# Rows added inside the output projection by an identity product, a shorter root chain, and four layer-norm tiles moved to ScalarE

## The reference

```python
def _layernorm(x, axis=-1, eps=1e-05):
    m = jnp.mean(x, axis=axis, keepdims=True)
    v = jnp.var(x, axis=axis, keepdims=True)
    return (x - m) / jnp.sqrt(v + eps)

x = x + _L0_attn_ref(_layernorm(x, axis=-1), ...)            # "own", causal, 16 heads; ends in out @ out_w + out_b
x = x + _L0_xattn_ref(_layernorm(x, axis=-1), ctx_1024, ...) # "cross", 154 keys; ends in out @ Wo + bo
x = x + _L0_ffn_ref(_layernorm(x, axis=-1), ...)             # "feed", quantised, with a depthwise convolution
x = x + _L1_attn_ref(_layernorm(x, axis=-1), ...)            # "second", 16 heads; ends in out @ w_out.T + b_out
x = x + _L1_xattn_ref(_layernorm(x, axis=-1), ctx_1024, ...) # "wide", one head
x = x + _L1_ffn_ref(_layernorm(x, axis=-1), ...)             # experts, top 2 of 16, and a shared one
return x
```

## Time and profile before

| | us |
|---|---|
| median of 3 runs | 3818.49 (3815.27 to 3821.42) |
| the profiled execution | 3815.54 |
| its span, first to last instruction | 3814.1 |
| TensorE busy (products) | 3274.6 (86% of the span) |
| VectorE busy | 2484.7 (65%) |
| ScalarE busy | 1735.8 (46%) |
| GpSimd busy | 546.1 (14%) |
| mean granted TensorE clock | 0.886 of full |

### The profile page before, as it was taken

One profiled execution on the slowest core, in us unless ns is written; L12 is line 12 of the kernel. 1 busy time (PEld: TensorE's weight loads), 2 busy tenths in 40 slices (PEclk: granted clock), 3 DMA queues, 4 the chain that ended last, 5 costly groups with the idle time before them and its releaser, 6 DMA issues. The chain is left out here.

```text
span 3814.1 us, 47638 instructions
## 1 busy us (share of the span) xinstructions
PE 3274.6 (86%) x17904; PEld 1798.5 (47%) x17904; DVE 2484.7 (65%) x4712; ACT 1735.8 (46%) x2434; POOL 546.1 (14%) x990
## 2 busy tenths in 40 slices
PE   5997679979999768988999975998898977799889
PEld 3443332358644333236864433323686433322378
DVE  5856678646685577854667547884566755688456
ACT  2553436633345443653345444465334544546532
POOL 0111010014111101002401110100241010010033
PEclk8898779979989777998998977799898997789989
DMA  3211011013021101101312010110231111021022
GB/s 122 43 32 35 0 26 34 9 47 112 23 51 23 35 1 34 26 9 62 107 25 47 15 35 1 34 34 1 76 93 38 35 21 29 1 42 26 1 89 91
DMA packets 119366, 149.24 MB, mean 39 GB/s; under 512 B 25445, under 2 KB 77159, under 8 KB 118835
## 3 DMA queue, kind: packets, MB, share of 16 engines
q1 hardware_dynamic: 119115, 145.95, 15.9%
HBM read 75.46 MB, written 4.46 MB: 21 GB/s over the span
## 5 line engine op out<-in xcount | busy, mean ns | idle before, releaser
L694 DVE TENSOR_REDUCE small<-psum 128x1 f32<-128x512 f32 (+6 forms) x1856 | 1148.6, 657 | 332.3 <-PE psum L571 293.8
L660 ACT ACTIVATE work<-psum 128x1024 f32<-128x1024 f32 (+5 forms) x1024 | 921.4, 935 | 502.5 <-PE psum L598 252.5
L571 PE MATMUL psum<-work 96*128 96x512 bf16 (+4 forms) x2688 | 729.1, 341 | 137.8 <-issue 59.6
L1607 PE MATMUL psum<-rounded_work 128*128 128x512 f32 (+1 forms) x3456 | 621.0, 343 | 4.4 <-ACT work L1671 4.4
L594 PE MATMUL psum<-work 99*128 99x512 bf16 (+4 forms) x2048 | 590.0, 372 | 8.8 <-DMA work<-work 6.5
L1607 PEld LDWEIGHTS psum<-rounded_work 128*128 128x128 f32 x3456 | 543.5, 193 | 80.9 <-ACT work L1671 6.3
L571 PEld LDWEIGHTS psum<-work 96*128 96x128 bf16 x2688 | 244.7, 103 | 695.4 <-DVE small L694 362.8
L626 PE MATMUL psum<-work 128*32 128x512 f32 (+4 forms) x4480 | 545.9, 540 | 1.6 <-ACT work L660 1.4
L594 PEld LDWEIGHTS psum<-work 99*128 99x128 bf16 (+1 forms) x2048 | 182.7, 99 | 216.9 <-ACT work L660 64.8
L1679 ACT CAST rounded_work<-work 128x512 fp32r<-128x512 f32 x144 | 89.3, 620 | 352.1 <-DVE work L1714 324.6
L724 POOL CAST small<-small 128x16 bf16<-128x16 f32 x96 | 18.8, 196 | 1418.0 <-issue 1104.0
(11 more groups left out here) (271 smaller groups left out, 3914.4 us busy)
## 6 DMA issues: line engine op xcount, KB each, us to landing
work<-work SPq DMA_DIRECT2D x320, 192.0 KB, 4.3
work<-combine SPq DMA_DIRECT2D x64, 512.0 KB, 4.0
work<-in_w_gate SPq DMA_DIRECT2D x64, 128.0 KB, 3.5
work<-in_w_up SPq DMA_DIRECT2D x64, 128.0 KB, 3.4
work<-in_w_down SPq DMA_DIRECT2D x64, 128.0 KB, 3.8
work<-in_x SPq DMA_DIRECT2D x10, 512.0 KB, 5.0
out<-x SPq DMA_DIRECT2D x8, 512.0 KB, 2.9
work<-work SPq DMA_DIRECT2D x64, 28.9 KB, 2.0
```

The source lines that it names most:

```text
L571: ins = nc.tensor.matmul(dst[:, c * n:(c + 1) * n], A.q_pair[0:ROWS, slot, h, P * i:P * (i + 1)], A.k_of(pair, h)[0:ROWS, s0:s0 + n], star ...
L660: nc.scalar.activation(probs[0:size, n % 4, :, 0:P * many], banks(2 * (n % 2), 2)[0:size, :, 0:P * many], ACT.Exp, scale=DH ** -0.5).then_ ...
L694: nc.vector.tensor_reduce(tops[:, pair % 2, places[0]:places[-1] + 1:step], src, AX.X, ALU.max) \
L1607: ins = nc.tensor.matmul(dst, a_parts[i], b_parts[j], start=start and n == 0, stop=stop and n == 2, skip_group_check=True)
```

## The change

- Out projections: GpSimd's sum leaves `x` plus bias in `x` as before. TensorE now multiplies two tiles of it at a time by the identity (`rows_tensor`, 128 by 512 float32) into bank j with `start=True`, and the projection's products of both tiles are accumulated on top. Four such products: the first ahead of the last pair's spin, the second behind it, the third behind the last turn, the fourth ahead of the last two tiles. VectorE takes the statistics straight from PSUM, and ScalarE copies each finished bank to `x` (`sum_scalar`). VectorE's adds are gone, and so are TensorE's waits for them, in `cross_tensor` and `wide_tensor` too.
- Root chain: variance plus epsilon is folded into ScalarE's square root (scale 0.25 and a bias of epsilon/4, which makes half the root), and the refining step into two combined instructions; the clamp, one sum and one halving go. This holds for every norm.
- The first four tiles of the norms own, cross, feed and second are normed by ScalarE (`norm_rows_scalar`, Identity with a scale and a bias per partition), after VectorE has written -mean times rstd for the half (mark `scaled`). ScalarE's order is given in `out_scalar`.
- GpSimd's bias sums of cross and second are issued after its top part of pair 2 in these heads.
- The marks are regrouped on semaphores `vector_norm` and `scalar_norm`.

```diff
 def norm_half(tag, i0, rows=None):
+    norm_variance(tag, i0, HT)
+    norm_root(tag, i0, HT)
+    if by_scalar(tag, i0):
+        nc.vector.scalar_tensor_tensor(out=root_parts(i0, HT)[1], in0=mean_of(i0, HT), scalar=-1.0, in1=rstd[:, i0:i0 + HT],
+                                       op0=ALU.mult, op1=ALU.mult).then_inc(*up("vector_norm", "scaled", tag))
+    else:
+        for j in range(i0, i0 + HT):
+            norm_rows(tag, j, rows)
...
-            own(ins)
-            nc.vector.tensor_scalar(root_parts(i0, n)[2], variance_of(i0, n), LN_EPS, None, ALU.add).then_inc(*up("variance", tag, i0))
+            ins.then_inc(*up("vector_norm", "variance", tag, i0))
...
-            dve.wait_ge(*at("root", tag, i0))
-            own(nc.vector.tensor_scalar(s0, s0, 1e-18, None, ALU.max))
+            dve.wait_ge(*at("scalar_norm", "root", tag, i0))
             own(nc.vector.reciprocal(s1, s0))
-            own(nc.vector.tensor_tensor(s1, s1, s2, ALU.mult))
-            own(nc.vector.tensor_tensor(s0, s0, s1, ALU.add))
-            own(nc.vector.tensor_scalar(s0, s0, 0.5, None, ALU.mult))
+            own(nc.vector.scalar_tensor_tensor(out=s2, in0=variance_of(i0, n), scalar=LN_EPS, in1=s1, op0=ALU.add, op1=ALU.mult))
+            own(nc.vector.scalar_tensor_tensor(out=s0, in0=s2, scalar=0.25, in1=s0, op0=ALU.mult, op1=ALU.add))
             own(nc.vector.reciprocal(rstd[:, i0:i0 + n], s0))
...
+        def norm_rows_scalar(tag):
+            act.wait_ge(*at("vector_norm", "scaled", tag))
+            for j in range(HT):
+                if tag in SUMMED:
+                    act.wait_ge(*at("added", tag, j // 2))
+                nc.scalar.activation(xn[:, j, :], x[:, j, :], ACT.Identity, scale=rstd[:, j:j + 1], bias=root_parts(0, HT)[1][:, j:j + 1]) \
+                    .then_inc(*up("scalar_norm", "normed", tag, j))
...
                 elif kind == "spin":
                     pair, = key
+                    if pair == PAIRS_OF_HEADS - 1:
+                        rows_tensor(A, 0)
...
                     ins.then_inc(*up("spun", a, pair))
+                    if pair == PAIRS_OF_HEADS - 1:
+                        rows_tensor(A, 1)
...
+                    if pair == 2 and bias is not None:
+                        out_gpsimd(A, bias)
...
+        def rows_tensor(A, j):
+            if j == 0:
+                pe.wait_ge(*at("filled", A.tag))
+            nc.tensor.matmul(bank(j), ident[:, :], x[:, 2 * j:2 * j + 2, :].rearrange("p i d -> p (i d)"), start=True, stop=False, skip_group_check=True)
+
         def out_tensor(A, tag, w):
+            rows_tensor(A, 2)
             pe.wait_ge(*at("out_turned", A.tag, 1, 1))
-            for i in range(NT):
-                if i >= 4:
-                    pe.wait_ge(*at("added", tag, i - 4))
-                project(bank(4 + i % 4)[:, 0:D], lambda k: oT[:, k, P * i:P * (i + 1)], w).then_inc(*up("out_projected", tag, i))
+            for j in range(NT // 2):
+                if j == 3:
+                    rows_tensor(A, 3)
+                for i in (2 * j, 2 * j + 1):
+                    for k in range(KD):
+                        ins = nc.tensor.matmul(bank(j)[:, D * (i % 2):D * (i % 2 + 1)], oT[:, k, P * i:P * (i + 1)], w[:, k, :],
+                                               start=False, stop=(k == KD - 1), skip_group_check=True)
+                ins.then_inc(*up("out_projected", tag, j))
...
+        def out_vector(tag):
+            for j in range(NT // 2):
+                dve.wait_ge(*at("out_projected", tag, j))
+                norm_stats(2 * j, bank(j)[:, 0:D])
+                own(nc.vector.bn_stats(stats[:, 6 * (2 * j + 1):6 * (2 * j + 2)], bank(j)[:, D:2 * D]), "vector_norm", "counted", tag, j)
+                if j % 2:
+                    norm_half(tag, 2 * j - 2)
+
+        def out_scalar(tag, turn):
+            sum_scalar(tag, 0)
             root_scalar(tag, 0)
+            sum_scalar(tag, 1)
+            norm_rows_scalar(tag)
             if turn:
                 turn_scalar(tag, 0)
                 turn_scalar(tag, 1)
+            sum_scalar(tag, 2)
             root_scalar(tag, 1)
+            sum_scalar(tag, 3)
             if turn:
                 turn_scalar(tag, 2)
                 turn_scalar(tag, 3)
+
+        def sum_scalar(tag, j):
+            act.wait_ge(*at("vector_norm", "counted", tag, j))
+            nc.scalar.copy(x[:, 2 * j:2 * j + 2, :].rearrange("p i d -> p (i d)"), bank(j)).then_inc(*up("added", tag, j))
...
             root_scalar("feed", 0)
+            norm_rows_scalar("feed")
+            turn_scalar("feed", 0)
+            turn_scalar("feed", 1)
             root_scalar("feed", 1)
-            for j in range(NT // 2):
-                turn_scalar("feed", j)
...
-            out_gpsimd(cross_heads, resident["cross_ob"][:, :])
-            heads_gpsimd(cross_heads)
+            heads_gpsimd(cross_heads, resident["cross_ob"][:, :])
```

More of the change, by code:

```diff
@@ L334, in setup_vector @@
             nc.vector.memset(rounders[:, 1:2], -ROUND)
+            own(nc.vector.memset(rounders[:, 2:3], LN_EPS / 4))
             dve.wait_ge(*at("feed_loaded", 1))
@@ L375, in root_parts, with by_scalar, normed, norm_half @@
             return [small[:, base + j * n:base + (j + 1) * n] for j in range(3)]
+        SHARED_NORMS = ("own", "cross", "feed", "second")
+        SUMMED = ("own", "cross", "second")
+        def by_scalar(tag, j):
+            return tag in SHARED_NORMS and j < HT
+        def normed(tag, j):
+            return at("scalar_norm" if by_scalar(tag, j) else "vector_norm", "normed", tag, j)
         def norm_vector(tag, i, rows=None):
-            norm_stats(i, rows)
+            norm_stats(i, (x if rows is None else rows)[:, i, :])
             if (i + 1) % HT == 0:
-                norm_variance(tag, i + 1 - HT, HT)
-                norm_root(tag, i + 1 - HT, HT)
-                for j in range(i + 1 - HT, i + 1):
+                norm_half(tag, i + 1 - HT, rows)
+        def norm_half(tag, i0, rows=None):
+            norm_variance(tag, i0, HT)
[5 more added lines that the diff above has]
+                for j in range(i0, i0 + HT):
                     norm_rows(tag, j, rows)
-        def norm_stats(i, rows=None):
+        def norm_stats(i, row):
             dve.wait_ge(m.sem("dve_step"), m.count.get("dve_step", 0))
-            nc.vector.bn_stats(stats[:, 6 * i:6 * i + 6], (x if rows is None else rows)[:, i, :]).then_inc(*up("dve_step"))
+            nc.vector.bn_stats(stats[:, 6 * i:6 * i + 6], row).then_inc(*up("dve_step"))
         def norm_variance(tag, i0, n):
@@ L812, in norm_scalar, with out_gpsimd @@
                 turn_scalar(tag, 3)
+        def sum_scalar(tag, j):
+            act.wait_ge(*at("vector_norm", "counted", tag, j))
+            nc.scalar.copy(x[:, 2 * j:2 * j + 2, :].rearrange("p i d -> p (i d)"), bank(j)).then_inc(*up("added", tag, j))
+        def out_gpsimd(A, bias, rows=None):
+            nc.gpsimd.tensor_tensor(x[:, :, :], x[:, :, :] if rows is None else rows, spread(bias, 1, NT), ALU.add).then_inc(*up("filled", A.tag))
+        def norm_scalar(tag):
+            for half in range(2):
+                root_scalar(tag, half)
+                turn_scalar(tag, 2 * half)
+                turn_scalar(tag, 2 * half + 1)
         lines = xn[:, :, :]
@@ L1791, in scalar_program @@
             heads_scalar(own_heads)
-            norm_scalar("own", True)
+            out_scalar("own", True)
             cross_scalar()
             heads_scalar(cross_heads)
-            norm_scalar("cross", False)
+            out_scalar("cross", False)
             feed_scalar()
@@ L1798, in scalar_program @@
             heads_scalar(second_heads)
-            norm_scalar("second", True)
+            out_scalar("second", True)
             wide_scalar()
@@ L1805, in vector_program @@
             heads_vector(own_heads)
-            out_vector(own_heads, "own")
+            out_vector("own")
             cross_vector()
             heads_vector(cross_heads)
-            out_vector(cross_heads, "cross")
+            out_vector("cross")
             feed_vector()
@@ L1812, in vector_program @@
             heads_vector(second_heads)
-            out_vector(second_heads, "second")
+            out_vector("second")
             wide_vector()
```

49 lines of the change are left out of this document (21 added, 28 removed).

## The result

| | before | after |
|---|---|---|
| median (4 runs each) | 3817.36 | 3750.14 (3744.52 to 3751.78) |
| ratio, 95% interval | | 0.9821 (0.9810 to 0.9833) |
| the profiled execution | 3815.54 | 3751.41 |
| its span | 3814.1 | 3750.1 |

The change makes the kernel 67.2 us faster by the medians, 64.0 in span between the two profiled executions. Forecast were 3756.5 us and 62 in the profiled execution.

The account below looks back on a forecast made before the run. Short serial stretches at out projections and norms, one engine working while others wait, were taken to bound the kernel. Terms sum to -15.2 a batch, -62 with setup, giving 3753.5 profiled and 3756.5 us median; range 3741 to 3777.

Parts of the forecast that it names:

- Bias sum: Start of the cross heads: moving GpSimd's sum frees the blocked VectorE copy, so cross heads start earlier, -4.3 us a batch.
- The lower end (0): Cost to VectorE of the bias sum at its new place: taken as 0, upper end 8.6 us a batch.
- Cross: Cross out projection: VectorE's chain done at 408.15 instead of 413.89, identity products holding the clock, -5.7 us a batch.
- Rival 1: Cross projection: the clock falls all the same, 2.8 us a batch lost, 3768 us; chance 0.20.
- Own: Own out projection: cross query products start at 292.05 against 291.87, +0.2 us a batch (-0.1 to +1.2).
- Feed: Feed norm: fewer small instructions and four rows gone from VectorE, -2.3 us a batch, lower end -1.4.
- Second: Second out projection: ScalarE's order binds, wide products start at 769.5 instead of 771.68, -2.1 us a batch (-1.1 to -2.8).
- Wide: Wide norm: shorter root chain gives 0.4 in the first half and 0.6 in the second, -1.0 us a batch.
- Rival 4: Wide: the clock stays up, last three tiles keep their earlier pace, 2 us a batch, 3748.5 us; chance 0.04.
- Setup: Setup ahead of the batches: has the shorter root chain twice, -1.2 us once.
- Rivals 2, 3 and 5: ScalarE binds (3767, chance 0.10); bias sum blocks VectorE in heads (3791, 0.04); clock falls in own and second (3837, 0.02).

Follow-up runs that it names:

- experiment 1: Kernel before with only GpSimd's bias sums of cross and second moved behind its top part of pair 2: 3791.57 against 3816.04 us, ratio 0.9938.
- experiment 2: Kernel before plus three unread identity products per out projection, ahead of the last spin, behind it and ahead of the projection: 3808.54 us, ratio 0.9975.
- experiment 3: Kernel before with the shorter root chain alone (lines 394, 399 and 403 folded away): 3787.25 us, ratio 0.9931.
- experiment 5: Changed kernel with VectorE again norming the first four tiles in own, cross, feed and second: 3755.11 us, ratio 0.9842.
- experiment 6: Changed kernel with all four identity products behind the last turn, each ahead of its pair of tiles, leaving the gaps empty: 3774.99 us, ratio 0.9891.
- the second execution: Changed kernel run once more, unaltered, for a second profiled execution: 3746.53 us, ratio 0.9823.

## Why the prediction was right

- **Bias sum**, -4.3: measured -4.28 to -4.35, and alone in experiment 1. The lower end (0) for its new place was the right one.
- **Cross**, -5.7: measured -5.66, the reduction 11.91 behind the projection's start against 11.8. Taken apart by experiments: 2.75 is the clock (2), 1.04 the root chain (3), 0.13 the split (5); by difference 1.7 is left for the adds, which no run takes away alone. The clock's share was -2.8 in the forecast. The forecast lets the projection start at 396.35, 0.13 earlier than before, without giving the step (the 0.18 of the first product alone would make it 396.66); measured, it starts 0.15 earlier behind the last value, 4.70 instead of 4.85 us: the turn ahead of it takes 1.09 instead of 1.44. Rival 1 falls in all four batches of both executions. The rule of the Trainium skill ("TensorE: Matmul & The Clock Gate", Part 4: transposes don't count for the clock) is in line with experiment 2, but these gaps held idle time as well as transpositions, and with empty gaps the clock stayed up in two batches of experiment 6; what the transpositions alone do can't be read from them.
- **Own**, +0.2: measured +0.46. ScalarE's rows take 0.52 each, not 0.44 (the upper bound was 0.69), and the root with scale and bias 0.30 instead of 0.20 and 0.36 instead of 0.27 to reach VectorE. The query products start 9.93 behind the projection, not 9.6.
- **Feed**, -2.3: measured -2.29 between its first turn and the second query product. The first half gave nothing of its own: what the root chain saved there (0.52 in experiment 3) ScalarE's later rows took back. The forecast had the right sum.
- **Second**, -2.1: measured -2.62 in three batches, -1.94 in the fourth. The queue behind the turns is as forecast, and the last turn starts 1.96 earlier behind the last value, against 2.1. The rest, 0.67, is the clock of that turn (1.30 instead of 1.97 us), which the forecast had left out; it isn't had in batch 4 of the first execution. The window over the last turns in before,

```profile
762.40:771.70 9.30, 3.29 (x17) 2.42 (x17) 6.54 (x25) 2.56 (x5) 0.00 (x0) 0.75 0.00 0
```

  and in after:

```profile
752.00:758.00 6.00, 2.35 (x17) 1.41 (x15) 3.20 (x14) 3.85 (x8) 0.00 (x0) 0.97 0.00 0
```

- **Wide**, -1.0: measured -1.02 to -1.25; the idle time of the earlier trace rows is 2.37 instead of 3.03. Rival 4 fell: without filling, the clock is at 0.60 over its end.
- **Setup**, -1.2: +0.35 in one execution, -0.96 in the other, +0.29 with the root chain alone and -0.74 in experiment 1, which leaves the setup as it was. A start differs by as much between executions, so the term isn't confirmed.
- **Left out**: behind the shorter waits of feed and second the stretch at 1.2 GHz is shorter too: 4.1 instead of 8.6 us between the second query products and the second score, 3.1 instead of 5.6 in the wide query products (batch 1). That gave -4.6 and -5.1. It is no general rule, and the length of the wait alone doesn't set it: in experiment 6 feed's waits are those of the changed kernel, and there it is 8.2 us again in front of the second score; the wait ahead of the cross heads is shorter in all four batches, and their time at the lower clock fell in two. The heads, where the clock's changes only moved, gave +5.8 in all (own +8.2, cross -4.2, second +1.8). With the rest they came to -2.6; in the second execution the own heads lost 3.7 instead of 8.2. So the mechanisms that the forecast names for its stages held, but that the total was met as closely is in part luck: a term was missing whose parts reach 8 us, and that they cancelled is chance.
- **Rivals 2, 3 and 5** fell: by experiment 5, by experiment 1, and by the own and second projections' pace (32 records as 5.45 and 1.89).

## What to carry to other kernels

Look at a wait of TensorE twice: for its length, and for the stretch behind it at the lower clock; here the second part cost time only where TensorE's own products gate what follows. Products that nobody reads, put into such waits, are worth trying: in this kernel they gave nearly as much (61 us) as the whole change (67 us), and nothing at the start of the cross heads, where TensorE's pace doesn't gate. Before crediting a saving on an instruction, look for one whose duration differs from its twins: a copy ten times its usual length beside another engine's instruction cost 4.3 us a batch, more than all the small instructions that the shorter root chain takes out of a stage (1.04). And before crediting a stretch to an edit, run the same program twice: where the length depends on when the clock changes, one profile can show 2 to 3 us that the other doesn't.

## What the runs showed of the hardware

- A bias sum of GpSimd (float32, 128x2048, 4.94 us there and 4.52 beside the maxima) holds up a bf16 copy of VectorE from SBUF to SBUF almost to its own end (4.71 against 0.41) and leaves maxima that read PSUM untouched (0.64 before, beside and behind it).
- ScalarE's square root of 128x4 takes 0.30 with a scale of 0.25 and a bias read from SBUF and 0.20 without, and VectorE, which waits for it, is idle for 0.36 instead of 0.27.
- Identity with a scale and a bias per partition took 0.52 a row of 256 columns out of SBUF in a run of four.
- Where the granted clock changes differs between two executions of one program: the own heads of batch 1 took 154.7 and 151.5 us, with the same work on every engine.
